# Moving the q and k projection to transposed form, with a trip through DRAM and a new order of turns, in an attention and feed-forward layer

## The reference, cut to what matters

```python
h = layernorm(x)
q, k, v = split(h @ w_qkv + b_qkv)          # 16 heads of 16
q, k = q*cos + rotate_half(q)*sin, the same for k
score = softmax(where(causal, q @ k.T / 4, -9e15))
x = x + (score @ v) @ w_o + b_o
w_t = clip(round(w_f / mean(abs(w_f))), -1, 1)
x = x + layernorm(x) @ (w_t * mean(abs(w_f))).T + b_f
```

## Time and profile before

| | |
|---|---|
| median of 3 runs | 273.57 us (272.15 to 277.85) |
| span of the profiled execution, first to last instruction | 275.7 us |
| TensorE busy | 254.3 us, 92% |
| VectorE, ScalarE, GpSimd busy | 178.1, 124.5, 108.6 us |
| mean granted TensorE clock | 0.975 |

### The profile page before, as it was taken

One profiled execution on the slowest core, in us unless ns is written; L12 is line 12 of the kernel. 1 busy time (PEld: TensorE's weight loads), 2 busy tenths in 40 slices (PEclk: granted clock), 3 DMA queues, 4 the chain that ended last, 5 costly groups with the idle time before them and its releaser, 6 DMA issues.

```text
span 275.7 us, 5793 instructions
## 1 busy us (share of the span) xinstructions
PE 254.3 (92%) x1968; PEld 182.3 (66%) x1968; DVE 178.1 (65%) x396; ACT 124.5 (45%) x244; POOL 108.6 (39%) x195
## 2 busy tenths in 40 slices
PE   0497999999999999999999999999999999989875
PEld 0164757766877687768776877687768776656533
DVE  1918588789677767776777677767776776430241
ACT  2403423636554645464546454645464543264100
POOL 2422140347138514751385147513851473065030
PEclk9999999889999999999999999999999999995997
DMA  6930000000000000000000000000000000000101
GB/s 219 303 109 0 2 1 0 7 0 2 5 2 2 32 12 2 2 31 10 2 0 31 9 2 0 32 9 2 0 31 10 2 0 31 15 0 0 40 0 38
DMA packets 6105, 6.88 MB, mean 25 GB/s; under 512 B 427, under 2 KB 5675, under 8 KB 6092
## 3 DMA queue, kind: packets, MB, share of 16 engines
q1 hardware_dynamic: 5804, 5.92, 6.5%
q10 hardware_dynamic: 288, 0.79, 0.8%
HBM read 4.34 MB, written 2.10 MB: 23 GB/s over the span
## 4 chain that ended last, share of the span: by engine, by line
PE 83%; DVE 9%; DMA 2%; POOL 2%; ACT 1%; issue 1%; POOLq 0%; SPq 0%
PE a_ps L807 16%; PE score_ps L875 15%; PE c_ps L941 12%; PE pv_ps L922 9%; PE score_ps L871 8%; PE scoret_ps L900 7%; PE a_ps L858 4%; PE score_ps L858 3%; PE c_ps L773 3%; DVE xn L547 2%; DMA xs<-in_L_attn_x 2%; PE c_ps L932 2%; PE a_ps L828 1%; PE score_ps L790 1%; PE a_ps L773 1%
## 5 line engine op out<-in xcount | busy, mean ns | idle before, releaser
L494 ACT ACTIVATE probs<-scoret_ps 128x512 f32<-128x512 f32 x96 | 52.4, 602 | 48.0 <-PE scoret_ps L900 47.8
L671 DVE TENSOR_REDUCE neg_max<-score_ps 128x2 f32<-128x512 f32 (+1 forms) x96 | 62.8, 684 | 14.6 <-PE score_ps L875 14.5
L395 POOL TENSOR_SCALAR_AFFINE_SELECT probs<-probs 128x256 f32<-128x256 f32 (+1 forms) x96 | 46.9, 507 | 23.1 <-ACT probs L494 22.2
L875 PE MATMUL score_ps<-k_t,q_t 48*128 48x128 f32 (+1 forms) x256 | 53.0, 307 | 0.0
L385 POOL TENSOR_SCALAR rstd<-mean_var 128x2 f32<-128x2 f32 x17 | 3.3, 192 | 114.8 <-DVE mean_var L556 114.8
L875 PEld LDWEIGHTS score_ps<-k_t,q_t 48*128 48x128 f32 x256 | 35.4, 185 | 16.5 <-issue 9.8
L900 PE MATMUL scoret_ps<-q_t,k_t 64*128 64x256 f32 (+1 forms) x256 | 37.3, 306 | 0.4 <-ACT probs L494 0.4
L871 PE MATMUL score_ps<-mask_bf,ident_bf 128*128 128x256 bf16 (+1 forms) x96 | 30.7, 319 | 0.7 <-DVE neg_max L671 0.3
L900 PEld LDWEIGHTS scoret_ps<-q_t,k_t 64*128 64x128 f32 x256 | 27.2, 192 | 5.2 <-issue 3.0
L922 PE MATMUL pv_ps<-probs,v 128*32 128x128 f32 (+1 forms) x512 | 26.7, 339 | 0.4 <-POOL probs L395 0.4
L485 ACT CAST q_t<-a_ps 128x512 fp32r<-128x512 f32 x16 | 9.3, 583 | 27.3 <-PE a_ps L858 27.3
(11 more groups left out here) (109 smaller groups left out, 469.7 us busy)
## 6 DMA issues: line engine op xcount, KB each, us to landing
xs<-in_L_attn_x SPq DMA_DIRECT2D x8, 256.0 KB, 7.7
out_y<-xs SPq DMA_DIRECT2D x8, 256.0 KB, 2.2
wqkv<-in_L_attn_w_qkv ACTq DMA_DIRECT2D x2, 384.0 KB, 4.7
qkv_bias<-in_L_attn_b_qkv SPq DMA_DIRECT2D x1, 384.0 KB, 6.5
wo<-in_L_attn_w_o SPq DMA_DIRECT2D x1, 256.0 KB, 6.7
wf<-in_L_ffn_weight SPq DMA_DIRECT2D x1, 256.0 KB, 8.1
q_t<-max_t SPq DMA_DIRECT2D x16, 16.0 KB
const<-in_consts SPq DMA_DIRECT2D x1, 176.0 KB, 4.6
```

The source lines that it names most:

```text
L395: nc.gpsimd.affine_select(out=blk, in_=blk, compare_op=ALU.is_ge, fill=0.0, base=0, pattern=[[0, blk.shape[1]], [1, P]], channel_multiplie ...
L494: nc.scalar.activation(probs[n // 6][:, n % 6, :], scoret_ps[n % 2][:], ACT.Exp).then_inc(exp_done, 1)
L671: nc.vector.tensor_reduce(neg_max[:, t, r, pairs.start:pairs.stop], score_ps[r][:].rearrange("p (h k) -> p h k", k=keys), AX.X, ALU.max, n ...
L875: last = mm(dst[:, i * keys:(i + 1) * keys], q_t[a.slot][rows, u, t * P:(t + 1) * P], k_t[a.slot][rows, u, 0:keys], start=False, stop=u == ...
```

## The change

The weights' columns are sorted on the host so that the transposed product comes out with half a head's features in each group of rows. `qk_project(z, j)` makes q (j = 0) or k (j = 1) of all 256 tokens with features on the partitions: 12 products of 256 columns each, w as the stationary operand. Their bias is added in `rope_products`, now with `scalar_tensor_tensor`. The rotated parts are split into `parts_h` and `parts_l` of 128 x 512, written to a DRAM tensor by three transfers of 256 KB for each j (`parts_to_rows`), and read back by two of 384 KB each (`rows_to_keys`) into the 48 rows of `q_t` or `k_t`. The 32 transposes of `qk_transpose` and their 8 copies go. `q_t`, `k_t` and `v` have three slots and no longer two. v's bias is folded into the output's bias once.

The mask of the first pass is now two products of 64 rows, in the same half of the rows as the fill's heads. `session(a, b, m)` issues the fills of both passes alternately, instruction by instruction, the first pass in one half of TensorE's rows and the second in the other. The ternary weights are kept as -1, 0 and 1 in FP32R, xn2 is split into a high and a low part, and the scale is applied in `output`. Both normalisations are applied on ACT, and `inverse_deviation` has four instructions on POOL and no longer two. `rope_sum` of j = 0 is on POOL and of j = 1 on DVE. The loop is gone; all turns are written out. The products of zeros go except eight at the start. All lists are new:

```diff
-            with eng.Fori(0, LOOPS) as pair: ...
+            for turn in range(TURNS):           # TensorE
+                z, a, b, c = turn, turn - 1, turn - 2, turn - 3
+                do(b, maxima_transpose)
+                do(c, values, 3)
+                do(c, o_transpose)
+                do(z, xn_transpose)
+                session(a, b, 0)
+                do(c, attn_transpose)
+                do(z, qk_project, 0)
+                session(a, b, 1)
+                do(c, attn_project)
+                do(z, qk_project, 1)
+                session(a, b, 2)
+                do(z, v_project)
+                session(a, b, 3)
+                do(b, values, 0)
+                do(c, xn2_transpose)
+                session(a, b, 4)
+                do(b, values, 1)
+                do(c, ternary_linear)
+                session(a, b, 5)
+                do(b, values, 2)
```

```diff
+    VectorE: split_maxima(b); first_statistics(z); normalise_attention(c, 0), (c, 1); xn_low(z);
+      maxima(a, 0); rope_products(z, 0); maxima(a, 1); residual(c); second_statistics(c);
+      rope_products(z, 1); rope_sum(z, 1); maxima(a, 2); qk_low(z, 0); qk_low(z, 1); maxima(a, 3);
+      xn2_low(c); maxima(a, 4); output(c); maxima(a, 5)
+    ScalarE: first_normalise(z); o_copy(c, 1); max_t_copy(b); xn_high(z); fill_rows (turns 0 to 2);
+      exps(b, 0); attn_t_copy(c); exps(b, 1); v_copy(z); exps(b, 2); second_normalise(c);
+      qk_high(z, 0); exps(b, 3); qk_high(z, 1); xn2_high(c); exps(b, 4); o_copy(b, 0); exps(b, 5)
+    GpSimd: deviation(z); deviation2(c); causal(b, 0); add_bias2(c); causal(b, 1); rope_sum(z, 0);
+      causal(b, 2); causal(b, 3); add_bias(b); causal(b, 4); causal(b, 5)
+    SyncE: move_maxima(b); parts_to_rows(z, 0), (z, 1); rows_to_keys(z, 0), (z, 1); store(c)
```

```diff
+            def rows_to_keys(z, j):
+                wait(sp, parts_out[j], 48 * (z + 1))
+                wait(sp, scoret_done, FILLS * (z - SLOTS + 1))
+                for r in range(2):
+                    dst = (q_t, k_t)[j][z % SLOTS]
+                    sp.dma_start(dst[ROWS * r:ROWS * r + PROD, :, :].rearrange("p u s -> p (u s)").bitcast(F32),
+                                 scratch[z, j, :, :, r * ROWS:(r + 1) * ROWS].rearrange("w e (i u) s -> (w e) i (u s)", u=PAIRS)
+                                 ).then_inc(qk_in[z % SLOTS], 16)
...
+            def session(a, b, m):
+                has_a, has_b = 0 <= a < B, 0 <= b < B
+                if has_a and m == 0:
+                    wait(pe, qk_in[a % SLOTS], 64 * (a // SLOTS + 1))
+                if has_b and m == 0:
+                    wait(pe, max_rows[b % SLOTS], 32 * (b // SLOTS + 1))
+                for n in (2 * m, 2 * m + 1):
+                    many, many_t = len(score_fill(n)[2]), len(scoret_fill(n)[2])
+                    if has_a:
+                        wait(pe, max_done, FILLS * a + n - 1)
+                        score_mask(a, n, False)
+                    if has_b:
+                        wait(pe, exp_done, FILLS * b + n - 1)
+                        score_t(b, n, 0)
+                    if has_a:
+                        score_mask(a, n, True)
+                    for i in range(max(many, many_t)):
+                        if has_a and i < many:
+                            score(a, n, i)
+                        if has_b and i + 1 < many_t:
+                            score_t(b, n, i + 1)
```

More of the change, by code:

```diff
@@ L58, with do, once @@
 MASKED = -9e15
[L60 to L104, removed]
+SCALE = HD ** -0.5
+C_COS, C_SIN, C_ID = 0, S, 3 * S
+C_MASK, C_SHIFT = C_ID + P, C_ID + 2 * P
+C_BIAS = C_SHIFT + P + HALF_Q
+C_END = C_BIAS
+def do(n, step, *args):
+    if 0 <= n < B:
+        step(n, *args)
+def once(now, step, *args):
+    if now:
+        step(*args)
 def wait(eng, sem, value):
-    if not isinstance(value, int) or value > 0:
+    if value > 0:
         eng.wait_ge(sem, value)
[L113 to L118, removed]
 def spread(ap, axis, n):
@@ L428, in turn @@
                 do(b, causal, 1)
+                do(z, rope_sum, 0)
                 do(b, causal, 2)
+                do(b, causal, 3)
                 do(b, add_bias)
-                do(first(z), fill_constants)
-                do(z, rope_sum, pool, 0)
-            turns(pool, turn)
+                do(b, causal, 4)
+                do(b, causal, 5)
         @block.scalar
@@ new lines, in fill_rows @@
+            def fill_rows(i):
+                if i == 0:
+                    act.wait_ge(ones_made, 1)
+                for r in range(2):
+                    rows = slice(ROWS * r + 2 * HD, ROWS * (r + 1))
+                    nc.scalar.copy(q_t[i][rows, 0, 0:P], ones[rows, :]).then_inc(rows_filled, 1)
+                    nc.scalar.copy(k_t[i][rows, :, :].rearrange("p u (a s) -> p (u a) s", s=P),
+                                   spread(ones[rows, :], 1, 2 * PAIRS)).then_inc(rows_filled, 1)
@@ L811, in xn_transpose, with keep_warm, start_warm, ternary_scale @@
-            def xn_transpose(a):
-                wait(pe, xn_made, a.count(1, 1))
-                if first(a):
+                last.then_inc(sig, 1)
+            def keep_warm(n):
+                for _ in range(n):
+                    mm(c_ps[:], zeros_bf[:, 0:P], zeros_bf[:], start=True, stop=True)
+            def start_warm():
+                pe.wait_ge(zeros_made, 1)
+                keep_warm(8)
+            def ternary_scale():
+                pe.wait_ge(wf_step, 1)
+                pe.wait_ge(ones_made, 1)
+                mm(c_ps[:, D:D + 1], ones[:], wf_abs[:, 0:1], start=True, stop=True).then_inc(wf_sum_ps, 1)
@@ L1043, with columns @@
+    return table
+def columns():
+    order = []
+    for part in range(2):
+        for half in range(2):
+            for row in range(P):
+                r, i, u = row // ROWS, row // PAIRS % HALF, row % PAIRS
+                order.append((2 * u + r) * 3 * HD + part * HD + half * HALF + i)
+    order += [h * 3 * HD + 2 * HD + d for h in range(H) for d in range(HD)]
+    return np.array(order)
 def kernel(**inputs):
```

956 lines of the change are left out of this document (413 added, 543 removed).

## The result

| | before | after |
|---|---|---|
| median | 275.66 us (272.15 to 277.85, 4 runs) | 382.27 us (376.28 to 383.94, 4 runs) |
| span of the profiled execution | 275.7 us | 381.1 us |
| TensorE busy | 254.3 us | 236.4 us |
| mean granted TensorE clock | 0.975 | 0.70 |

Medians are over all runs, which for one kernel lie up to 3 per cent apart, and a ratio compares the faster runs of both kernels. The ratio is 1.387, interval [1.369, 1.404]. The change makes the kernel slower, as forecast, but by 107 us where 43 were forecast, and the time lies outside the range of 288 to 350.

What follows compares the result with a forecast made beforehand. TensorE bound the kernel at 27.57 us a turn; new waits and a lower clock make it 33.5. Against 275.7: +29.6 for five intervals, +5, +8, start and tail slightly less: 319, as median 317 us (305 to 330; with rivals 288 to 350).

Steps and rivals of the forecast that it cites:

- the trip through DRAM: Stores and loads of q and k on SP's queue: 7.7 us, ending at 26, hidden by the turn's other waits.
- S0: Start of the next turn's session 0, the zero point of the forecast's times within a turn.
- The rival of few engines: Loads spread over six of 16 engines take 10.6 us, 2 to 3 us a turn more: 340 us, chance 0.30.
- The head: Turn's start, session 0 waiting for the maxima's rows: chain of 8.3 us, TensorE idle for 5.4 of it.
- T5: End of session 5 in a turn; forecast at 23.3 us after S0.
- POOL's list: POOL work queued behind deviation2 delays rope_sum to 15.2 and session 4 to 18.6 us, a stall of some 4 us.
- The clock's +2: TensorE at 1.2 GHz after gaps, for session 0, attn_transpose and q's projection: 2 us a turn, from 31.6 to 33.5.
- TensorE's own work: TensorE's instructions in a full turn fall from 27.57 to 22.4 us, if it never waits.
- not yet covered: Turns 1 to 3: each sequence's first trip not yet hidden, the two intervals 28 us each, +8 in all.
- the clock stays up: Rival: dense sessions keep TensorE's clock from falling: 298 us (288 to 305), chance 0.16.
- the waits are short: Rival: session 0 and POOL are not held, the turn falls to TensorE's 22.4 us: 239 us, chance 0.07.
- equal: Rival: the waits in a turn are half their forecast size: 272 us, chance 0.05.

Runs made afterwards that it cites:

- The run without the loads: Changed kernel with rows_to_keys left out from the fourth sequence on (3 to 7), stores kept: 351.51 us, ratio 1.292.
- the fastest version: Changed kernel with the trip one turn earlier, loads over 16 engines, new lists, add_bias last, three plus five products of zeros: 267.85 us, ratio 0.977.
- the version without zeros: Changed kernel with the trip one turn earlier, contiguous loads over 16 engines and new lists, products of zeros taken out: 279.67 us, ratio 1.010.
- the order alone: Changed kernel with only the lists of ACT, DVE and POOL reordered: 366.79 us.
- the zeros alone: Changed kernel with only products of zeros added in TensorE's waits (10, 30 and 8): 369.76 us.
- the same four repairs: Loads over 16 engines, reordered lists, add_bias last, zeros: 355.97 us on the changed kernel, 293.51 us on it with the trip one turn earlier.

## Why the prediction was wrong

The failed step is **the trip through DRAM, "I take it as hidden"**. I ended the loads at 26 us after S0 by the 395 GB/s of the start; measured, k's last part left DVE at S0 + 20.8 (18 forecast; 1.0 of the 2.8 is the DVE instruction beside POOL's), the first load was issued at 216.11 and the last had landed at 233.31, S0 + 38.6: 17.2 us for the four, where I took 5.5. The bound that I had beside it ("they last 19 us, end at 39 and make the turn 5.5 longer") was right to half a microsecond in its end, in part by luck, since it began the loads 1 us too early and made them 2 us too long; and its turn, 33.5 + 5.5 = 39.0, is what five intervals between full turns took: 197.6 / 5 = 39.5 (first mask of session 0 at 112.97 and at 310.55). I set it aside "since the start's loads shared the engines with eight others". That reason was an argument, the 4.7 us was a row.

**The rival of few engines** named the mechanism and the window shows it (0.37, 123 GB/s), but it missed the second limit, the 48 rows (10.6 us forecast for the four loads, 17.2 measured), and it priced the consequence at 2 to 3 us a turn, 340. The run without the loads sizes it: 5.4 us a turn (39.5 against 34.1), 27 over the five.

**The list of terms, where the trip is away** (the run without loads):
- The head, T5 to S0, 8.3 forecast: session 5 ended at 201.59, session 0 began at 210.47: 8.9.
- POOL's list, rope_sum ended at S0 + 15.2 forecast: 14.6; session 4 at S0 + 18.6 forecast: 195.55 - 176.41 = 19.1. T5 at S0 + 23.3: 25.2.
- The clock's +2: the turn was 31.6 + 2 = 33.5 forecast, 34.06 measured. Size and sum hold; that they hold separately is not shown.
- TensorE's own work, 22.4 us: in the fastest version's turn at a granted clock of 1.00, 22.94 busy less the eight zeros, 1.83 in its chain, is 21.1; the version without zeros has 21.16 busy in a turn. The sessions were still cheaper than I took them: the rows left "passes side by side" open, and it does what it says.

**The sum.** Against the profiled 319 stand 381.1. The five full intervals give (39.5 - 33.5) x 5 = +30. The two intervals of turns 1 to 3 were 28 each in the forecast and were 71.4 together (first mask of session 0 at 41.59, 76.24, 112.97): +15. The start should have gained 1; the first mask came at 41.59, and at 30.46 before: +12. What is left, 5, is the tail. So 27 of the 62 us lie in the start, where I had priced one trip "not yet covered" at a few microseconds: the first three sequences have little beside their trip, and each trip is 19 us long. Not all of it is fixed: the run without the loads changes nothing up to there, and its third session 0 began at 105.99 and not 112.97. The step from the span to the median, 319 to 317, had no ground either: in every run here the time is about 2 us above the span (383.2 and 381.1), and the profiled 275.7 belonged to a run of 277.8.

"Rivals: the clock stays up", "the waits are short", "equal" were all on the wrong side. "TensorE busy near 75%" was 62%, and 64% in the run without the loads, so the loads made only a part of the idle time. "The loads from DRAM as the releaser at a turn above 38" is what I had named as the sign of a wrong prediction, and it is what the profile shows.

**Where the change's gain went.** TensorE's work fell from 27.57 to 21.1 us a turn, more than forecast, and the change as it stands turned it into waits: the loads of five sequences about 29 us of the 107 (26 by the ratios, 31 by the medians); the rest are the first three trips, the lists and the clock they bring, whose parts can't be added (the order alone 15 us, the zeros alone 12). With the trip one turn earlier, new lists and eight zeros, a full turn is 23.7 us and the kernel 2.3 per cent, 7 us, faster than before. In the profiled executions the five intervals behind the third session 0 gain 20 us (118.0 against 137.9) and the end 2; the start takes back 13, for in a pipeline of twelve turns, not eleven, the first session 0 begins at 43.41 and not 30.46.

## What to carry to other kernels

When a change replaces work of a busy engine by a trip through memory, write down the ring it closes, and price every transfer in it by its shape, not its bytes: blocks, rows and halves set the rate, and a row at the worst rate is the value to take until something excludes it. Count the issues too: a layout that needs more transfers can cost on the queue what it saves in the load. If the ring is longer than the turn, change the distance in the pipeline first; the same four repairs were worth 26 us ahead of that and 47 behind it. In a list without a gap on the matrix engine, a microsecond saved by opening one cost over four, three of them by the clock.

## What the runs showed of the hardware

- 384 KB into 48 rows: 6.86 us from six blocks, 4.35 from 48 rows, 2.77 into 128 rows. Two such loads into the two halves took 5.96 to 6.79 on one queue and 6.72 to 6.88 on two.
- A DVE instruction of 512 columns with two SBUF inputs took 1.70 us and no longer 0.69 beside a POOL `tensor_tensor`.
- The issue of a store of 128 KB kept SP for some 0.65 us when several followed one another (four in 2.59; twelve in 8.5).
- A gap of 1.15 us in an otherwise gapless turn was followed by a granted clock of 0.50 with TensorE busy throughout (156 to 161 us), and in two turns of the same run by 1.00. In the changed kernel the clock was 1.00 from 184 to 186 with TensorE busy for 0.78 of 2 us, and 0.50 from 195 to 199 with TensorE busy all the time: the busy share of a stretch does not tell its level.
- Side by side the passes were cheaper than any bound I had (8 us for the twelve fills of each): in session 2 of the changed kernel, at the full clock, the masks of two fills of two heads start 0.35 us apart with both passes in it, and the whole session takes 0.91 us (204.95 to 205.86); they start 0.64 apart for the first pass alone before.

```profile
204.95 0.28 PE L674 MATMUL score_ps<-mask_bf,shift_bf 64*128 64x256 bf16 x1
...
205.30 0.28 PE L674 MATMUL score_ps<-mask_bf,shift_bf 64*128 64x256 bf16 x1
```
